# A two-layer adaLN model on one NeuronCore: more contracted rows in the first layer's attention, its maxima one step earlier, and another engine for one copy

## The reference

```python
h = layernorm(x) * (1 + ca) + sa
latent = h @ Wc_down                       # 128 -> 64
q = (latent @ Wq_up).reshape(B, T, 16, 8)  # 16 heads of 8
kv = latent @ Wkv_up; k, v = kv[..., :8], kv[..., 8:]    # one k, v for all heads
att = einsum('bthd,bsd->bhts', q, k) / sqrt(8)
att = softmax(where(causal, att, -inf))
y = einsum('bhts,bsd->bthd', att, v).reshape(B, T, C)
x = x + ga * (y @ Wc_proj)
```

## Time and profile before

| | |
|---|---|
| median of 3 runs | 948.38 us |
| lowest, highest | 939.05, 956.61 us |
| the profiled execution | 954.41 us |
| its span, first to last instruction | 952.7 us |
| mean granted TensorE clock | 0.875 of 2.4 GHz |
| busy over the span | TensorE 84%, VectorE 58%, ScalarE 47%, GpSimd 42% |

### The profile page before, as it was taken

How to read it: one execution, slowest core, us unless ns; L and a number is a source line. 1 busy time by engine, 2 the same in 40 slices (tenths; PEclk the granted TensorE clock), 3 DMA queues, 4 the chain that set the end, 5 groups by cost and what they waited for, 6 DMA issues and landing times.

```text
span 952.7 us, 22934 instructions
## 1 busy us (share of the span) xinstructions
PE 801.5 (84%) x9158; PEld 405.7 (43%) x9158; DVE 553.2 (58%) x1503; ACT 449.8 (47%) x726; POOL 399.6 (42%) x531
## 2 busy tenths in 40 slices
PE   4577988898989899988688999988985778999887
PEld 3223333334343334424334444443433445666555
DVE  2574656656666565715577533330248758888875
ACT  1003545435454455655232433333324858888663
POOL 5101012323232230321000688878755569886423
PEclk9656979869797788989599998887995989999999
DMA  5730343244344123122300133333330011111111
GB/s 138 132 71 9 89 131 86 52 97 139 95 79 97 47 71 90 44 56 74 115 0 1 48 43 45 45 43 44 33 44 23 6 26 26 24 35 24 24 28 34
DMA packets 73838, 54.98 MB, mean 58 GB/s; under 512 B 23677, under 2 KB 66734, under 8 KB 73134
## 3 DMA queue, kind: packets, MB, share of 16 engines
q1 hardware_dynamic: 63878, 45.96, 19.8%
q0 software_dynamic: 9856, 7.58, 6.1%
HBM read 31.76 MB, written 18.23 MB: 52 GB/s over the span
## 4 chain that ended last, share of the span: by engine, by line
PE 49%; DVE 15%; POOL 12%; DMA 9%; issue 7%; ACT 3%; SPq 3%; POOLq 1%; DVEq 0%; ACTq 0%
POOL d_acc L1354 7%; PE bank L458 7%; PE ps_s L421 7%; PE bank L437 7%; DVE MX L854 3%; PE b1ps L2048 3%; PE ps_s L417 3%; DMA Q<-d_m 3%; PE b1ps L2059 3%; POOL XG L1344 3%; DMA d_m<-ms 2%; PE ps_o L1558 2%; PE b1ps L2072 2%; PE ps_h L1546 2%; DVE R L1450 1%
## 5 line engine op out<-in xcount | busy, mean ns | idle before, releaser
L854 DVE TENSOR_REDUCE MX<-bank 128x1 f32<-128x320 f32 (+13 forms) x352 | 185.7, 565 | 120.3 <-PE bank L465 119.4
L639 ACT ACTIVATE PR<-ps_s 128x1024 f32<-128x1024 f32 x160 | 160.4, 1023 | 169.5 <-PE ps_s L417 98.3
L458 PE MATMUL bank<-K,Q 72*32 72x32 bf16 (+15 forms) x2048 | 128.7, 330 | 31.7 <-DMA Q<-d_q 15.3
L421 PE MATMUL ps_s<-Q,K 75*32 75x512 bf16 (+1 forms) x1088 | 118.1, 423 | 16.2 <-DMA Q<-d_m 16.1
L458 PEld LDWEIGHTS bank<-K,Q 72*32 72x32 bf16 x2048 | 51.3, 109 | 113.4 <-issue 34.1
L437 PE MATMUL bank<-PR,VE 128*32 128x512 f32 x640 | 97.9, 693 | 0.0
L1354 POOL DMA_INDIRECT d_acc<-Y,idx x56 | 87.6, 1565 | 20.4 <-issue 16.5
L1558 PE MATMUL ps_o<-H,w 128*128 128x512 f32 x176 | 89.6, 660 | 0.0
L1344 POOL DMA_INDIRECT XG<-d_tab,idx x56 | 53.8, 961 | 78.6 <-DVE idx L1459 62.1
L1678 ACT ACTIVATE H<-ps_h,b1T 128x512 f32<-128x512 f32 x88 | 60.4, 687 | 42.3 <-PE ps_h L1546 39.9
L465 PE MATMUL bank<-maskQ,identb 128*32 128x32 bf16 (+3 forms) x1408 | 74.6, 207 | 0.0
(11 more groups left out here) (344 smaller groups left out, 1403.3 us busy)
## 6 DMA issues: line engine op xcount, KB each, us to landing
Q<-d_q SPq DMA_DIRECT2D x24, 384.0 KB
d_q<-qs SPq DMA_DIRECT2D x24, 128.0 KB, 2.4
X<-L_attn_x SPq DMA_DIRECT2D x8, 256.0 KB, 4.9
w<-L_ffn_W SPq DMA_DIRECT2D x8, 256.0 KB, 4.0
d_acc<-zrow SPq DMA_DIRECT2D x1, 2048.0 KB, 9.5
w<-L_ffn_W SPq DMA_DIRECT2D x1, 2048.0 KB, 9.6
AC<-d_acc SPq DMA_DIRECT2D x8, 256.0 KB, 2.9
d_y<-ysb SPq DMA_DIRECT2D x112, 18.0 KB
```

The lines of the kernel that those rows point to most:

```text
L421: last = nc.tensor.matmul(out_, k_[0:r, P * i + o:P * i + o + QW], q_[0:r, :, P * g + QW * j:P * g + QW * j + QW], start=True, stop=True, ...
L458: nc.tensor.matmul(mx[o:o + QW, x * w:(x + 1) * w], Q[b % QB][0:NPR, 4 * c + hh, QW * j:QW * j + QW], K[b % QB][0:NPR, 0:w], start=(x == 0 ...
L639: nc.scalar.activation(by_head.rearrange("p h (c x) -> p c h x", x=QW), ps_s[half][:, :].rearrange("p (c h x) -> p c h x", c=2, x=QW), ACT ...
L854: nc.vector.tensor_reduce(MX[b % 2][:, c:c + len(cs)], ring[R0.place["max", G]][:, 0:len(cs) * w].rearrange("p (x w) -> p x w", w=w), AX_X ...
```

## The change

- Contracted rows. The maxima's products and all unmasked scores use rows 0 to 96 (`KF` = 97) instead of 72 and 75; the diagonal matmuls use all 128 rows instead of 107; the wholly masked ones use 128 rows of `maskT` instead of one. Rows that must not count are zero on one side. Since rows 72 to 74 of Q hold the maxima of an earlier block, each block's are set to zero by one more DMA before q is loaded.
- The rows that are the same for all blocks are now 56 rows of K and 53 rows of Q (57 + 868 KB each). The three buffers are written at three places of SyncE's queue (`LIMIT_ROWS`), and each of the first three blocks' maxima wait for their own.
- Steps. hT, k, q, v move to steps 0 to 3, the maxima to steps 8 and 9 of round b-2 and 0 to 6 of round b-1, m to step 6 (behind h2). The parts on VectorE, GpSimd and SyncE move with them: the stores and loads of k and q to SyncE's steps 2 and 3, which puts them ahead of `rl`'s transfers at step 4, and m's to step 6.
- q's bank. ScalarE copies the bank to `qr` in float32, which frees it, and then rounds `qr` to the first part; VectorE subtracts in place.

```diff
-KQ = KM + QW
+KF = P - QW + 1
-HEAD_STEPS, BODY_STEPS = 1, 8
+HEAD_STEPS, BODY_STEPS = 2, 7
+LIMIT_ROWS = [(-2, 1), (-2, 7), (-1, 2)]
+QIN = 16 * (2 * PARTS + 1)
-MISC0 = {1: [("hT", 2)], 2: [("k", 2)], 3: [("q", 2)], 4: [("v", 2)], 6: [("h2", -2)],
-         7: [("lg", -2), ("m", 1)], 8: [("pj", -1)]}
+MISC0 = {0: [("hT", 2)], 1: [("k", 2)], 2: [("q", 2)], 3: [("v", 2)], 6: [("h2", -2), ("m", 1)],
+         7: [("lg", -2)], 8: [("pj", -1)]}
-    KC = sb0("KC", [PARTS + QW, T], BF16)
-    QC = sb0("QC", [QW, T], BF16)
+    KC = sb0("KC", [P - NPR, T], BF16)
+    QC = sb0("QC", [P - KM, T], BF16)
...
 # TensorE, scores
-                pe.wait_ge(s_kc, 32 * QB)
-                        last = nc.tensor.matmul(out_, maskT[0:1, QW:2 * QW], bc(identb[0:1, 0:1], [1, 512]),
+                        last = nc.tensor.matmul(out_, maskT[:, QW:2 * QW], bc(identb[:, 0:1], [P, 512]),
-                        r = KQ if i == g and kt == j else KM
+                        r = P if i == g and kt == j else KF
 # TensorE, maxima
-                    pe.wait_ge(DS[f"q_in{b % 2}"], 96 * (b // 2 + 1))
+                    pe.wait_ge(DS[f"q_in{b % 2}"], QIN * (b // 2 + 1))
+                    if b < QB:
+                        pe.wait_ge(s_kc[b], 32)
-                                         Q[b % QB][0:NPR, 4 * c + hh, QW * j:QW * j + QW],
-                                         K[b % QB][0:NPR, 0:w], start=(x == 0), stop=False, tile_position=(0, o),
+                                         Q[b % QB][0:KF, 4 * c + hh, QW * j:QW * j + QW],
+                                         K[b % QB][0:KF, 0:w], start=(x == 0), stop=False, tile_position=(0, o),
 # ScalarE, q
-                nc.scalar.activation(qs[:, 0, :], m[:, :], ACT.Copy).then_inc(S["q1_rdy"], 1)
+                    act.wait_ge(S["q3_rdy"], b)
+                nc.scalar.activation(qr[:, :], m[:, :], ACT.Copy).then_inc(S["misc_free"], 1)
+                act.wait_ge(S["misc_free"], M0.full((kind, b)))
+                nc.scalar.activation(qs[:, 0, :], qr[:, :], ACT.Copy).then_inc(S["q1_rdy"], 1)
 # VectorE, q
-                nc.vector.tensor_tensor(qr[:, :], m[:, :], qs[:, 0, :], ALU.subtract).then_inc(S["misc_free"], 1)
-                free((kind, b))
+                lk(nc.vector.tensor_tensor(qr[:, :], qr[:, :], qs[:, 0, :], ALU.subtract))
 # VectorE and GpSimd, norm of block n + 3
-                if 0 <= b < NB and (s == 9 or b == 0):
+                if 0 <= b < NB and (s == 8 or b == 0):
 # GpSimd: third part of k at s == 1 (was 2), of q at s == 2 (was 3)
 # SyncE
-                if n == -1 and s == 0:
+                if (n, s) in LIMIT_ROWS:
+                    i = LIMIT_ROWS.index((n, s))
                     sp.wait_ge(s_eye, 1)
-                    for i in range(QB):
-                        sp.dma_start(K[i][NPR:KQ, :], KC[:, :]).then_inc(s_kc, 16)
-                        sp.dma_start(Q[i][KM:KQ, :, :], bc(QC[:, :].unsqueeze(1), [QW, NH, T])).then_inc(s_kc, 16)
+                    sp.dma_start(K[i][NPR:P, :], KC[:, :]).then_inc(s_kc[i], 16)
+                    sp.dma_start(Q[i][KM:P, :, :], bc(QC[:, :].unsqueeze(1), [P - KM, NH, T])).then_inc(s_kc[i], 16)
-                if 0 <= b < NB and s == 3:      # store of k
+                if 0 <= b < NB and s == 2:
-                if 0 <= b < NB and s == 4:      # load of K, store of q, load of Q
+                if 0 <= b < NB and s == 3:
...
                     sp.wait_ge(DS[f"q_st{par}"], 48 * (b // 2 + 1))
+                    sp.dma_start(Q[b % QB][NPR:KM, :, :], bc(QC[0:PARTS, :].unsqueeze(1), [PARTS, NH, T])
+                                 ).then_inc(DS[f"q_in{par}"], 16)
-                if 0 <= b < NB and s == 7:      # store and load of m
+                if 0 <= b < NB and s == 6:
```

More of the change, by code:

```diff
@@ L304, in program @@
     s_mq = sem("block_mask_ready")
-    s_kc = sem("limit_rows_loaded")
+    s_kc = [sem(f"limit_rows_loaded{i}") for i in range(QB)]
     s_lw = sem("late_weights_loaded")
@@ L725, in misc @@
                 dve.wait_ge(S["q1_rdy"], b + 1)
-                if b >= 1:
-                    dve.wait_ge(S["q3_rdy"], b)
-                nc.vector.tensor_tensor(qr[:, :], m[:, :], qs[:, 0, :], ALU.subtract).then_inc(S["misc_free"], 1)
-                free((kind, b))
+                lk(nc.vector.tensor_tensor(qr[:, :], qr[:, :], qs[:, 0, :], ALU.subtract))
                 nc.vector.tensor_copy(qs[:, 1, :], qr[:, :]).then_inc(S["q2_rdy"], 1)
@@ L941, in gpsimd_part @@
                                    in_=KC[:, :].rearrange("r (a x) -> r a x", x=QW), compare_op=ALU.not_equal, fill=-BIG,
-                                   base=-PARTS, pattern=[[0, NQB], [-1, QW]], channel_multiplier=1))
+                                   base=NPR + 1 - KF, pattern=[[0, NQB], [-1, QW]], channel_multiplier=1))
         lk(nc.gpsimd.memset(KC[0:PARTS, :], -1.0))
@@ L946, in gpsimd_part @@
                                    in_=QC[:, :].rearrange("r (a x) -> r a x", x=QW), compare_op=ALU.is_ge, fill=0.0,
-                                   base=-1, pattern=[[0, NQB], [-1, QW]], channel_multiplier=1))
+                                   base=KM - KF, pattern=[[0, NQB], [-1, QW]], channel_multiplier=1))
         nc.gpsimd.drain().then_inc(s_eye, 1)
@@ L991, in gpsimd_part @@
                 b = n + 2
-                if 0 <= b < NB and s == 2:
+                if 0 <= b < NB and s == 1:
                     pool.wait_ge(S["k2_rdy"], b + 1)
                     nc.gpsimd.tensor_tensor(ks[:, 2, :], kr[:, :], ks[:, 1, :], ALU.subtract).then_inc(S["k3_rdy"], 1)
-                if 0 <= b < NB and s == 3:
+                if 0 <= b < NB and s == 2:
                     pool.wait_ge(S["q2_rdy"], b + 1)
@@ L1108, in sync_part @@
                     if b >= 2:
-                        sp.wait_ge(DS[f"q_in{par}"], 96 * (b // 2))
+                        sp.wait_ge(DS[f"q_in{par}"], QIN * (b // 2))
                     for i in range(NT):
```

## The result

The changed kernel takes 1020.39 us (median; 1013.76 to 1025.57), the kernel before on the same chip 950.75 (939.05 to 956.61): a ratio of 1.0773, 95% interval 1.0635 to 1.0911. The forecast was 908 us. The changed kernel is 70 us slower, and the whole of that is lost before the first scores.

The account below looks back on a forecast made before the run. TensorE was taken to bound rounds 0 to 7. Round 0 -3.6, rounds 1 to 5 -23, round 6 -9.6, round 7 -5.5, start +1: -41 us, giving 913.7 profiled, 908 median; range 892 to 926, wider 872 to 936.

Parts of the forecast that it names:

- The start: Before round 0: larger constant rows ahead of Q's first load cost 0 to 2 us, taken as +1.
- Rows 1 to 128: Diagonal steps: without one-row matmuls all run four abreast, 1.27 us less a step, 5.1 us a round.
- The clock: Mid-round on TensorE: more rows or denser diagonal steps end most low-clock time, worth 5 us (bounds 0 and 5.2).
- the rival in which rows do nothing to it: Rounds 0 to 7: row count leaves the granted clock unchanged, low stretches stay, +18 us, 926 us; chance 0.17.
- The waits removed: TensorE's waits for m's rows (16.1 us over seven rounds) and q's bank (10.1) go; 1.3 and 1.4 in round 3.
- The wait that takes their place: Step 8: TensorE waits 4 us for Q's load, then some 3 us for yn behind rc's store and rl.
- T: The end of q's product on TensorE in a round, from which the prediction counted times up to step 8 and beyond.
- Sum without the start's loss: The forecast's addition of round and start changes: -41 us, from the profiled 954.4 to 913.7, or 908 for the median.
- the forecast's own range: 892 to 926 us for the median, from the bounds of Q's landing and the rl chain, 3 us a round each way.
- the wider one: 872 to 936 us, meant to hold 8 in 10, taking in most of one rival below and another above.
- Those on the round's waits and clock: Rivals: new waits stay away, 865 to 870 us (0.20); rows don't change clock, 926 (0.17); waits bring low clock, 976 (0.06).

Follow-up runs that it names:

- e1: The changed kernel with its 53 constant rows of Q sent as two DMAs of 5 and 48 rows; 934.02 us, 0.9855 of the kernel before.
- e16: e1 without the zeroing DMA, the maxima's products again with 72 rows; 922.55 us, 0.9665 of the kernel before.
- e11: The kernel before with 64 contracted rows instead of one in the wholly masked matmuls; 945.65 us, ratio 0.9848.
- e12: The kernel before with 65 contracted rows instead of one in the wholly masked matmuls; 922.67 us, ratio 0.9600.
- e2: The kernel before with 128 contracted rows instead of one in the wholly masked matmuls, nothing else; 904.72 us, ratio 0.9588.
- e6: e3 without the zeroing DMA, the maxima's products again with 72 rows; 915.47 us, 0.9704 of the kernel before.
- e5: e2 with ScalarE's copy of q's bank added; 909.93 us, 0.9634 of the kernel before.
- e15: e2 with moved steps, q's store ahead of K's load, rc's store before it, rl's load between, and ScalarE's copy of q; 915.03 us, ratio 0.9611.
- e4: The kernel before with only the steps moved as in the change, row counts and q's copy as before; 958.85 us, ratio 1.0153.
- e3: The kernel before with only 97 and 128 rows, zeroing DMA and constant rows (as 5 and 48), old steps and q copy; 936.24 us, ratio 0.9877.

## Why the prediction was wrong, point by point

**The start** was taken as +1 us, because "the DMA engines are idle there for most of it". Idle engines were no help: the load of 53 rows uses one of them. This is the step that failed, +88.8 instead of +1, and it alone turns a gain into a loss: e1, with the same bytes as 5 and 48 rows, takes 81 us of it back at the start and 86 in all. The zeroing DMA is most of what is left of it: without it e16 starts at 80.1, which is the +1. The 53 rows stand in the diff, and no rival had it.

**Rows 1 to 128**: right in place and size, and what separates the kinds is now known. The first half was to lose 1.27 - 0.43, and did (0.44 in the changed kernel). But the prediction put it down to one row beside many; e11 and e12 show that 64 rows separate as one does, and 65 are enough.

**The clock**: half right. It rose, and rounds 1 to 5 of e2 are 6.6 us shorter each, of which four diagonal steps are up to 5.1; the changed kernel itself had 0.86 to 0.93 in these rounds. But more rows in the unmasked scores (75 to 97) did nothing that shows: e6's rounds are no shorter than e2's (43.7, 43.0). The masked products do act on the clock, even at 64 rows (e11), which speaks against the rival in which rows do nothing to it. That their rows are the cause is not shown, since e12 with 65 had less than e11; the mechanism stays open.

**The waits removed**: m's rows fell from 16.1 to 3.8, q's 10.1 went. Both as said. That the copy of q is worth 1.4 us a round was not shown: with waits behind it, e5 gained nothing, and e15 has 6 us in all, 0.6%.

**The wait that takes their place**: the place was right. Q's load goes out at T + 11.8 (forecast 12), TensorE arrives at T + 18.7 (18), Q's rows are there at T + 25.5 (22), yn starts at T + 29.4 (26). SyncE stands 11 us behind Q's load for rc's store, as round 1 of before had shown with m's. The mis-sized term here is the zeroing DMA, put at 0.4 us and found to cost some 2: without it e16's rounds are 2.5 us shorter, e6's 1.4 (both also have 72 rows in the maxima's products).

**Sum without the start's loss.** e1's median, 934, lies over the forecast's own range (892 to 926) and inside the wider one (872 to 936). Its profiled execution is 18 us over the 913.7 that the forecast gave for one: +7 at the start, +12 in rounds 1 to 5 (47.4 instead of 45), +1.5 and +1.8 in rounds 0 and 7, -0.7 in round 6, -3 behind them. e16 (922.6) takes away what zeroing cost.

**The rivals.** Those on the round's waits and clock were the right questions on the wrong part: e4 shows that the moves alone lose 1.5%, so of the parts of the change only the masked products were shown to pay.

## What to carry to other kernels

Before a new DMA is called free because the DMA engines are idle, look at its row count: the 53 rows here, a prime number, went over one engine, and what the queue issued next waited for it. Let matmuls that are to run abreast stand on one side of the step between 64 and 65 rows; one line did that here, and its 4% is about what the forecast gave the whole change. And when two waits end in the same step, taking one away is worth what the other leaves: read both in the view of waits before and after.

## What the runs showed of the hardware that was not expected

- 868 KB over 53 rows moved at 24 GB/s, some 36 us, with the DMA engines' mean busy share at 0.07; the issue of the DMA behind it lasted up to 38.51 us.
- Matmuls of 64 rows between those of 75 and 107 started 0.31 us apart at each change of kind; with 65 rows there was no such gap.
- 64 rows instead of one in the masked products, with the bursts still broken, raised the granted clock of rounds 1 to 5 from between 0.80 and 0.89 to between 0.89 and 0.96 (one profile each) and took 1.5% off the time (ratio 0.9788 to 0.9908). With 65 rows and closed bursts it was 0.82 to 0.94 (one profile).
- A small DMA of three rows ahead of three loads of 384 KB made their issues longer, 0.45 instead of 0.36 us in the median of 24, and in e3's round 2 2.43 instead of 1.14 us for the three.
